# Routed experts of a mixture layer: every gathered block of rows is turned by TensorE instead of every second one by DMA

## The chip, the cores and the metric

The kernel runs on one core of a Trainium2 chip. The metric is the device time of one execution in microseconds (us), lower is better. All times below are of this kernel on that core.

## The reference, cut to what matters

The input is x of 2 x 2048 tokens with 512 features. An attention part comes first (not touched by this change). The feed-forward part is a shared expert plus 16 routed experts, four of them chosen for each token:

```python
g = jnp.einsum('sc,ech->esh', xf, gate_w)      # xf: normalised rows, S=4096, c=512
u = jnp.einsum('sc,ech->esh', xf, up_w)        # 16 experts, h=128
h = jax.nn.silu(g) * u
hw = h * combine.T[:, :, None]                 # zero unless the expert was chosen
routed = jnp.einsum('esh,ehc->sc', hw, down_w)
return (shared_out + routed).reshape(B, T, C)  # added to x
```

## The kernel before

Each of the 4096 tokens goes to 4 experts, which makes 16384 pairs. They are sorted by expert into blocks of 128 rows (P = 128), each block with one expert; with the padding of 16 experts there are at most 143 blocks that can hold a row. The kernel before works through BLOCKS = 144, a multiple of four, so its last block is always padding.

The program has three stretches that matter here. In the first (to about 504 us) there are attention, routing and the shared expert for the first four of eight token blocks. Its last step is `shared_down(FIRST * SH - 1)`. The second is the routed stage, 144 blocks. The third handles the shared expert of the four later token blocks (`gate_up_at`, `down_at`, lines 1015 to 1050) while the routed results y are gathered back by token and added (`combine`).

Values are held as two 16-bit parts, high and low, so a gathered row is 1024 16-bit numbers, and each product takes three matmuls (`PARTS`: high by high, high by low, low by high). The steps of one routed block s are:

- GpSimd gathers 128 rows by token number from DRAM into one of four buffers `xg` (L1832), after copying the token numbers (L1820). The gather waits until the block four before has been turned.
- The block is turned, so that features lie on partitions. Even blocks: eight 128x128 turns on TensorE into a PSUM bank (`turn_rows`, L946), emptied by VectorE into `xgT` (`save_rows`, L1669). Odd blocks: one transposing DMA from `xg` to `xgT_odd`, on SP's queue (`turn_odd`, L576), in order with the y writes (`y_out`, L567).
- TensorE: gate and up, 12 matmuls of 256 columns (`gate_up`, L961), with weights picked by the expert number held in a register.
- ScalarE takes silu of gate (L1269); VectorE multiplies by up (L1683); ScalarE makes the high part (L1273); VectorE the low part (L1686); TensorE turns the two parts (`turn_h`, L972); VectorE empties them (`save_h`, L1675).
- TensorE: down, 3 matmuls of 512 columns (`down`, L980). ScalarE saves y (`save_y`, L1279) into one of two buffers `y_sb`, once the buffer's last write to DRAM is done. SP writes it to `y_dram` (L567).

Order on TensorE: a loop of 34 rounds of four blocks (`four`), with some blocks written out at either end. In a round, for n = 0 to 3 and s = 4i + 1 + n, it does the turns of an even block where n is odd, then gate/up of s + 1, the turns of h of s, and down of s - 1. Each round begins with a load of eight expert numbers into registers (L936). The other engines have loops of four blocks, GpSimd of eight, in matching order.

SP's queue also carries, among the first blocks, the last block of x1 + shared sum to DRAM (`x1s_out(3)`, L484), the DMA transposes of 512 rows of a later token block (`later_turned_in(5)`, L467) and an x1 block in (`next_x1_in(3)`, L480).

Of the kernel before, what the change touches and what calls it, by code (L numbers as in the profile page):

```python
# [27 lines left out]
F16 = mybir.dt.float16  # L28
# [4 lines left out]
P = 128  # L33
# [10 lines left out]
TB = 4  # L44
# [8 lines left out]
BLOCKS = (NP + E * (P - 1)) // P + 1  # L53
# [26 lines left out]
R_EXP, R_BLK, R_TRI = 0, E, E + BLOCKS  # L80
# [3 lines left out]
def constants():  # L84
# [17 lines left out]
    r[:, R_BLK:R_BLK + BLOCKS] = np.arange(BLOCKS)  # L102
# [23 lines left out]
def build(nc, x, ctxT, wk, wqT, wv, wo, biases, bo, cb, routerT, gu_w, dn_w, const, const_r, out):  # L126
    with ExitStack() as ctx:
# [53 lines left out]
        counted = view(o1 + 8 * KB, [BLOCKS])  # L181
# [19 lines left out]
        hot_blk = [view(o2 + 4 * KB + 2 * BLOCKS * TOP_E * i, [TOP_E, BLOCKS], F16) for i in range(3)]  # L201
        hot_blk.append(view(o1 + 8 * KB, [TOP_E, BLOCKS], F16))
# [3 lines left out]
        r_silu, r_h = view(o3 + 8 * KB, [2, H]), view(o3 + 9 * KB, [2, H])  # L206
# [16 lines left out]
        blocks_e = little(BLOCKS + 8, I32)  # L223
# [30 lines left out]
        token_of = little(BLOCKS, I32)  # L254
        pair_row = little(NP // P, F16)
        places16 = little(BLOCKS, F16)
# [90 lines left out]
        s_tx, s_txe = sem("even_rows_turned"), sem("even_rows_turned_saved")  # L347
        s_odd = [sem(f"odd_rows_turned{h}") for h in range(2)]
        s_rg, s_rs, s_rh = sem("routed_gate_up"), sem("routed_silu"), sem("routed_h32")
        s_rhh, s_rhl = sem("routed_h_hi"), sem("routed_h_lo")  # L350
        s_ht, s_hte, s_rd = sem("routed_h_turned"), sem("routed_h_turned_saved"), sem("routed_down")
        s_ye = sem("y_saved")
        s_yw = [sem("y_written0"), sem("y_written1")]
# [22 lines left out]
        def stage_of(n):  # L376

            return n % 2 if n < TB else 2 + n % 2

# [6 lines left out]
        def _(sp):  # L386
# [178 lines left out]
            def y_out(s, j):  # L565
                sp.wait_ge(s_ye, s + 1)
                sp.dma_start(item(y_tiles, s), y_sb[:, j, :]).then_inc(s_yw[j], 16)  # L567


            def turn_odd(h, gathered, used):  # L570

                settled(sp)
                sp.wait_ge(s_xg[2 * h + 1], gathered)
                if used is not None:
                    sp.wait_ge(s_rg, used)
                sp.dma_start_transpose(xgT_odd[:, h, :, :], xg[:, 2 * h + 1, :]).then_inc(s_odd[h], 16)  # L576

            def four_blocks(i):

                loop = not isinstance(i, int)  # L580
                gathered = sp.to_reg(16 * i + 16) if loop else 16 * i + 16
                for h in range(2):
                    used = 4 * i + (2 * h - 2)
                    turn_odd(h, gathered, sp.to_reg(used) if loop else used)
                    for r in (2 * h, 2 * h + 1):
                        y_out(4 * i - 4 + r, r % 2)

            sp.wait_ge(s_shl, FIRST * SH)
            for h in range(2):
                turn_odd(h, 16, None)  # L590

            four_blocks(1)
            x1s_out(FIRST - 1)
            four_blocks(2)
            later_turned_in(FIRST + 1)
            four_blocks(3)
            next_x1_in(FIRST - 1)
            with sp.Fori(4, BLOCKS // 4) as i:
                four_blocks(i)
            for s in range(BLOCKS - 4, BLOCKS):  # L600
                y_out(s, s % 2)
# [4 lines left out]
            for j in range(2):  # L606
                sp.wait_ge(s_yw[j], 16 * BLOCKS // 2)
# [21 lines left out]
        def _(pe):  # L629
# [223 lines left out]
            def tokens(u):  # L853

                for q in range(4):
                    pe.wait_ge(s_hot, 4 * u + q + 1)
                    for i in range(TOP_E):
                        last = mm(bank[6][:, 0:BLOCKS], hot_row[q][:, i, :], hot_blk[q][:, i, :],
                                  start=(u == q == i == 0), stop=(u == SH - 1 and q == 3 and i == TOP_E - 1))
                    last.then_inc(s_hot_used, 1)  # L860
# [64 lines left out]
            shared_down(FIRST * SH - 1)  # L925


            pe.wait_ge(s_sh32, FIRST * SH)
            pe.wait_ge(s_x1s, FIRST * TB)
            pe.wait_ge(s_whi_r, E)  # L930
            pe.wait_ge(s_wlo_r, E)
            pe.wait_ge(s_expert, 1)
# [7 lines left out]
            def turn_rows(u, j, fresh):  # L940

                pe.wait_ge(s_xg[2 * j], 16 * ((u >> 1) + 1))
                if not fresh:
                    pe.wait_ge(s_txe, u - 1)
                for n in range(2 * KC):
                    last = turn(bank16[j][:, n * P:n * P + P], xg[:, 2 * j, n * P:n * P + P], id16)  # L946
                last.then_inc(s_tx, 1)

            def gate_up(s, r, e, fresh):

                j, rows = r % 2, (xgT, xgT_odd)[r % 2]
                if r % 2:
                    pe.wait_ge(s_odd[r // 2], 16 * ((s >> 2) + 1))
                else:
                    pe.wait_ge(s_txe, (s >> 1) + 1)
                if not fresh:
                    pe.wait_ge(s_rh, s - 1)
                n = 0
                for xv, wp in PARTS:
                    for kc in range(KC):  # L960
                        last = mm(bank[2 + j][:, 0:2 * H], rows[:, r // 2, xv * KC + kc, :],  # L961
                                  only((gu_hi_r, gu_lo_r)[wp], e, slice(kc * 2 * H, (kc + 1) * 2 * H)),
                                  start=(n == 0), stop=(n == 3 * KC - 1))
                        n += 1
                last.then_inc(s_rg, 1)

            def turn_h(s, j, fresh):
                pe.wait_ge(s_rhl, s + 1)
                if not fresh:
                    pe.wait_ge(s_hte, s - 1)  # L970
                for v in range(2):
# [3 lines left out]
            def down(s, j, e, fresh):  # L975
                pe.wait_ge(s_hte, s + 1)
                if not fresh:
# [5 lines left out]

            e = experts(0)
            turn_rows(0, 0, True)
            gate_up(0, 0, e[0], True)
            turn_rows(1, 1, True)
            gate_up(1, 1, e[1], True)
            turn_h(0, 0, True)
            def four(i, first):  # L990
                e = experts(4 * i)
                for n in range(4):
                    s = 4 * i + 1 + n
                    if n % 2:
                        turn_rows(2 * i + 2 + n // 2, n // 2, False)
                    gate_up(s + 1, (n + 2) % 4, e[n + 2], False)
                    turn_h(s, (1 + n) % 2, first and n == 0)
                    down(s - 1, n % 2, e[n], first and n < 2)

            four(0, True)  # L1000
            with pe.Fori(1, BLOCKS // 4 - 1) as i:
                four(i, False)
            e = experts(BLOCKS - 4)
            gate_up(BLOCKS - 2, 2, e[2], False)
            turn_h(BLOCKS - 3, 1, False)
# [898 lines left out]
```

## Time and profile before

| what | value |
|---|---|
| median of 3 runs | 1177.35 us (1174.76 to 1182.57) |
| the profiled execution | 1182.4 us, of which the span is 1180.6 us |
| mean granted TensorE clock | 0.945 of full speed |
| TensorE busy | 1049.6 us of the span |
| VectorE busy | 633.7 us |
| ScalarE busy | 385.8 us |
| GpSimd busy | 433.2 us |
| DMA | 227.69 MB, mean 193 GB/s |

The span is counted from the first to the last instruction of the profiled execution; all positions in time below count from its start. PE is TensorE's matmuls, PEld its weight loads (which overlap them), DVE is VectorE, ACT ScalarE, POOL GpSimd, SP the queue that issues most DMAs. A name like L961 is line 961 of the kernel before. The tile names are short: `arena` is all of SBUF that the kernel uses and `bank` any PSUM bank, so the line tells more than the name.

### The profile page before, as it was taken

How to read it: one execution, taken by the hardware profiler on the slowest of the kernel's cores; microseconds unless marked ns; L12 is line 12 of the kernel's file. 1: busy time of each engine (PE TensorE's matmuls, PEld its weight loads, DVE VectorE, ACT ScalarE, POOL GpSimd, SP SyncE). 2: the span in 40 equal slices, each digit the busy share in tenths (PEclk: the TensorE clock that was granted, in tenths of full speed). 3: DMA queues.
4: the chain of work that ended last, by engine and by line, in shares of the span. 5: the costliest groups of instructions: out<-in, count | busy, mean ns of one | idle time of the engine just before them, and what ended most of it. 6: DMA issues, size and time to landing. Idle time of an engine off the chain costs nothing.

```text
span 1180.6 us, 21537 instructions
## 1 busy us (share of the span) xinstructions
PE 1049.6 (89%) x6596; PEld 614.6 (52%) x6597; DVE 633.7 (54%) x1473; ACT 385.8 (33%) x776; POOL 433.2 (37%) x508
## 2 busy tenths in 40 slices
PE   5797979999969688987899999998889789999998
PEld 5494544444424234554666767666666334444443
DVE  5634876655268989832344444444333447565555
ACT  4433423433445343122344444444334011111111
POOL 0303631121225233132344444444431746545440
PEclk8889969999999889988999999999999889999999
DMA  9713754658663324169999999999996966967451
GB/s 358 258 33 104 261 152 137 203 147 248 168 161 108 107 81 134 36 148 243 246 251 255 253 251 255 259 255 235 230 214 180 390 221 166 231 178 212 137 169 42
DMA packets 215318, 227.69 MB, mean 193 GB/s; under 512 B 143682, under 2 KB 152804, under 8 KB 213732
## 3 DMA queue, kind: packets, MB, share of 16 engines
q1 hardware_dynamic: 191716, 149.41, 44.5%
q0 software_dynamic: 23552, 77.61, 23.6%
q8 instruction: 31, 0.51, 0.2%
q14 instruction: 19, 0.16, 0.1%
HBM read 123.93 MB, written 69.49 MB: 164 GB/s over the span
## 4 chain that ended last, share of the span: by engine, by line
PE 65%; DMA 11%; DVE 9%; issue 8%; SPq 4%; ACT 2%; POOL 1%; DVEq 0%; POOLq 0%; ACTq 0%
PE bank L1025 14%; PE bank L961 12%; PE bank L825 10%; PE bank L1037 7%; PE bank L837 6%; PE bank L980 5%; DMA arena<-arena 5%; DMA arena<-xr_dram,arena 3%; PE bank L946 2%; PE bank L713 2%; DVE arena L1647 1%; DMA arena<-in_x 1%; PE bank L635 1%; SPq L467 1%; PE bank L972 1%
## 5 line engine op out<-in xcount | busy, mean ns | idle before, releaser
L961 PE MATMUL bank<-arena 128*128 x1728 | 226.8, 281 | 37.7 <-DMA arena<-arena 20.3
L961 PEld LDWEIGHTS bank<-arena 128*128 128x128 f16 x1728 | 165.4, 99 | 92.1 <-issue 57.4
L825 PE MATMUL bank<-arena 128*128 128x512 f16 x768 | 181.8, 392 | 17.4 <-ACT arena L1213 7.8
L1853 POOL DMA_INDIRECT arena<-y_dram,arena x128 | 131.5, 1027 | 123.7 <-DVE arena L1722 68.8
L1025 PE MATMUL bank<-arena 128*128 128x512 f16 x768 | 174.4, 383 | 2.3 <-issue 1.9
L1832 POOL DMA_INDIRECT arena<-xr_dram,arena x144 | 141.5, 983 | 59.6 <-issue 45.5
L825 PEld LDWEIGHTS bank<-arena 128*128 128x128 f16 x768 | 76.6, 100 | 124.0 <-issue 28.6
L1683 DVE SCALAR_TENSOR_TENSOR arena<-bank,arena 128x128 f32<-128x128 f32 x144 | 42.0, 292 | 179.5 <-ACT arena L1269 134.7
L1025 PEld LDWEIGHTS bank<-arena 128*128 128x128 f16 x768 | 75.5, 98 | 97.8 <-issue 9.0
L980 PE MATMUL bank<-arena 128*128 x432 | 117.9, 382 | 1.7 <-issue 0.8
L1279 ACT ACTIVATE arena<-bank 128x512 f32<-128x512 f32 x144 | 84.8, 589 | 74.8 <-DMA y_dram<-arena 66.7
L1219 ACT ACTIVATE arena<-arena 128x512 f16<-128x512 f32 x64 | 40.4, 631 | 210.2 <-DVE arena L1464 108.4
L1722 DVE SCALAR_TENSOR_TENSOR arena<-arena 128x512 f32<-128x512 f32 x128 | 95.9, 750 | 18.8 <-DMA arena<-y_dram,arena 15.4
L1820 POOL COPY arena<-arena 128x1 int32 (+1 forms) x144 | 27.7, 192 | 204.9 <-DMA arena<-arena 121.5
L1037 PE MATMUL bank<-arena 128*128 128x512 f16 x384 | 90.8, 386 | 9.0 <-issue 9.0
L837 PE MATMUL bank<-arena 128*128 128x512 f16 x384 | 94.7, 400 | 0.0
L1269 ACT ACTIVATE arena<-bank 128x128 f32<-128x128 f32 x144 | 39.8, 277 | 117.6 <-PE bank L961 95.8
L1807 POOL TENSOR_TENSOR arena<-arena 128x1024 f32 x16 | 36.1, 2254 | 102.0 <-ACT arena L1228 91.1
L1686 DVE TENSOR_TENSOR arena<-arena 128x128 f16<-128x128 f32 x144 | 42.3, 293 | 54.3 <-ACT arena L1273 46.7
L1774 POOL TENSOR_TENSOR arena<-arena 128x2048 f16<-128x2048 f32 x7 | 28.5, 4073 | 105.6 <-ACT arena L1168 105.6
L1037 PEld LDWEIGHTS bank<-arena 128*128 128x128 f16 x384 | 38.0, 99 | 55.4 <-issue 12.0
L1730 DVE SCALAR_TENSOR_TENSOR arena<-bank,arena 128x512 f32<-128x512 f32 x32 | 22.1, 691 | 80.3 <-PE bank L1025 57.8
(205 smaller groups left out, 1327.8 us busy)
## 6 DMA issues: line engine op xcount, KB each, us to landing
y_dram<-arena SPq DMA_DIRECT2D x144, 256.0 KB
arena<-in_x SPq DMA_DIRECT2D x8, 1024.0 KB, 14.3
xr_dram<-arena SPq DMA_DIRECT2D x16, 512.0 KB, 3.0
x_dram<-arena SPq DMA_DIRECT2D x8, 1024.0 KB, 4.9
arena<-x_dram SPq DMA_DIRECT2D x8, 1024.0 KB, 6.0
arena<-in_gu_w SPq DMA_DIRECT2D x16, 512.0 KB, 3.4
out<-arena SPq DMA_DIRECT2D x32, 256.0 KB
arena<-in_gu_w POOLq DMA_DIRECT2D x8, 512.0 KB, 3.9
```

Source lines behind the costliest of these rows:

```text
L825: last = mm(bank[half][:, :], (gu_hi_s, gu_lo_s)[wp][:, c, at:at + H], xt[:, xv * KC + kc, :], start=(n == 0), stop=(n == 3 * KC - 1))
L837: last = mm(bank[2 + t][:, :], s_hb[:, g % 2, hv, t * P:t * P + P], (dn_hi_s, dn_lo_s)[wp][:, c, :], start=(c == 0 and n == 0), stop=(c == ...
L961: last = mm(bank[2 + j][:, 0:2 * H], rows[:, r // 2, xv * KC + kc, :], only((gu_hi_r, gu_lo_r)[wp], e, slice(kc * 2 * H, (kc + 1) * 2 * H) ...
L980: last = mm(bank[6 + j][:, :], r_hT[:, j, hv, :], only((dn_hi_r, dn_lo_r)[wp], e), start=(n == 0), stop=(n == 2))
L1025: last = mm(bank[GATE_UP[n % 2][g]][:, :], (gu_hi_s, gu_lo_s)[wp][:, c, at:at + H], xt[:, xv * KC + kc, :], start=(m == 0), stop=(m == 3 * ...
L1037: last = mm(bank[2 + t][:, :], s_hb[:, n % 2, hv, t * P:t * P + P], (dn_hi_s, dn_lo_s)[wp][:, c, :], start=(c == 0 and m == 0), stop=(c == ...
L1279: A(y_sb[:, j, :], bank[6 + j][:, :], ACT.Copy, scale=1.0 / WS).then_inc(s_ye, 1)
L1683: V.scalar_tensor_tensor(r_h[:, j, :], bank[2 + j][:, H:2 * H], 1.0 / WS, r_silu[:, j, :], ALU.mult, ALU.mult).then_inc(s_rh, 1)
L1686: V.tensor_tensor(r_hb[:, j, 1, :], r_h[:, j, :], r_hb[:, j, 0, :], ALU.subtract).then_inc(s_rhl, 1)
L1722: V.scalar_tensor_tensor(acc, ybuf[n % RING][:, e, :], w, acc, ALU.mult, ALU.add).then_inc(s_cmb, 1)
L1832: pool.indirect_dma_start(out=xg[:, r % 4, :], out_offset=None, in_=xr_dram[:, :], in_offset=bass.IndirectOffsetOnAxis(ap=token_now[:, r:r ...
L1853: pool.indirect_dma_start(out=ybuf[n % RING][:, e, :], out_offset=None, in_=y_dram[:, :], in_offset=bass.IndirectOffsetOnAxis(ap=row_of[:, ...
```

## The change

- Every gathered block is turned by TensorE, and VectorE empties each. The DMA transposes of the routed stage, `xgT_odd` and their semaphores go.
- On TensorE the turns of block s + 2 come ahead of gate/up of s + 1, the turns of h of s, and down of s - 1. The turns of blocks 0 and 1 come ahead of the last shared down projection. The first gate/up groups wait for the first quarters of the shared sum rather than for all.
- TensorE's routed stage has no loop; it is written out block by block, and loads the expert numbers every eighth block.
- y has four buffers instead of two. Two of them lie where the shared expert's silu is kept, so ScalarE waits for their last writes ahead of the last stage.
- 143 blocks instead of 144; tables of block numbers keep an even number of columns.
- The loops of ScalarE, VectorE, GpSimd and SP have eight blocks a round.

```diff
-BLOCKS = (NP + E * (P - 1)) // P + 1
+BLOCKS = (NP + E * (P - 1)) // P
+COLUMNS = BLOCKS + BLOCKS % 2
+UNROLLED = 8
+LOOPED = BLOCKS // UNROLLED - 1
...
-        xgT_odd = view(o1, [2, 2 * KC, P], F16)
-        y_sb = view(o3 + 4 * KB, [2, D])
+        y_sb = [view(v, [D]) for v in (o1, o3 + 4 * KB, o3 + 6 * KB, o1 + 2 * KB)]
...
-                sp.dma_start_transpose(xgT_odd[:, h, :, :], xg[:, 2 * h + 1, :]).then_inc(s_odd[h], 16)
...
+            for s in range(UNROLLED):
+                y_out(s, s % 4)
+                if s == 3:
+                    x1s_out(FIRST - 1)
+                    later_turned_in(FIRST + 1)
+                if s == 7:
+                    next_x1_in(FIRST - 1)
+            with sp.Fori(1, LOOPED + 1) as i:
+                for n in range(UNROLLED):
+                    y_out(UNROLLED * i + n, n % 4)
...
+            def turn_rows(s):
+
+                pe.wait_ge(s_xg[s % 4], 16 * (s // 4 + 1))
+                if s >= 2:
+                    pe.wait_ge(s_txe, s - 1)
+                for n in range(2 * KC):
+                    last = turn(bank16[s % 2][:, n * P:n * P + P], xg[:, s % 4, n * P:n * P + P], id16)
                 last.then_inc(s_tx, 1)
...
-            e = experts(0)
-            turn_rows(0, 0, True)
-            gate_up(0, 0, e[0], True)
...
-            four(0, True)
-            with pe.Fori(1, BLOCKS // 4 - 1) as i:
-                four(i, False)
...
+            turn_rows(0)
+            pe.wait_ge(s_sh32, FIRST * SH)
+            turn_rows(1)
+            shared_down(FIRST * SH - 1)
+            pe.wait_ge(s_expert, 1)
+            of = {s: e for s, e in enumerate(experts(0))}
+            gate_up(0, of[0])
+            for s in range(BLOCKS + 1):
+                if s + 2 < BLOCKS:
+                    turn_rows(s + 2)
+                if s + 1 < BLOCKS:
+                    gate_up(s + 1, of[s + 1])
+                if s % 8 == 5 and s + 3 < BLOCKS:
+                    of.update(enumerate(experts(s + 3), s + 3))
+                if s < BLOCKS:
+                    turn_h(s)
+                if s:
+                    down(s - 1, of[s - 1])
...
-            def gather(s, r, fresh, last):
-
-                if not fresh:
-                    if r % 2:
-                        pool.wait_ge(s_odd[r % 4 // 2], 16 * (s >> 2))
-                    else:
-                        pool.wait_ge(s_tx, (s - 2) >> 1)
+            def gather(s, r):
+
+                if not isinstance(s, int) or s >= 4:
+                    pool.wait_ge(s_tx, s - 3)
```

## Rows read from the trace of the kernel before

**Rows 1.** Stretches: us, busy us (instructions) by engine, granted clock, DMA share, GB/s
```profile
504.40:580.00 75.60, 56.95 (x443) 41.66 (x444) 24.91 (x75) 21.64 (x60) 24.64 (x43) 0.86 0.87 207
580.00:800.00 220.00, 206.95 (x1796) 151.42 (x1794) 93.48 (x300) 94.83 (x257) 100.62 (x173) 1.00 0.97 255
800.00:908.70 108.70, 94.79 (x792) 68.51 (x791) 41.14 (x133) 42.52 (x115) 38.31 (x64) 0.97 0.89 221
908.70:1180.60 271.90, 255.39 (x1152) 113.30 (x1150) 147.77 (x208) 39.70 (x65) 131.47 (x128) 0.97 0.65 192
```

**Rows 2.** Chain that ended last, 703 to 716 us: start us, us, what
```profile
703.09 0.45 PE bank L946 x8
703.54 1.31 PE bank L961 x12
704.85 0.11 PE bank L972 x2
704.96 0.65 PE bank L980 x3
705.61 0.51 issue
706.12 1.59 PE bank L961 x12
...
715.56 0.75 issue
```

**Rows 3.** Line 936, the register loads: duration ns min/median/max, first and last start
```profile
L936 PEldq TENSOR_LOAD <-arena x37: 587/712/1406, 507.0 to 900.7; - x37
```

**Rows 4.** Waits of TensorE, 504 to 909 us: us in total, times, longest
```profile
PE bank L961 <- DMA arena<-arena: 20.3, 8, 5.0
...
PE bank L961 <- DVE arena L1683: 3.7, 7, 0.8
PE bank L946 <- issue: 3.5, 1, 3.5
PE bank L961 <- DVE arena L1669: 1.9, 2, 1.0
PE bank L972 <- DVE arena L1686: 1.8, 4, 0.7
```

**Rows 5.** Order of time on TensorE, one group behind a DMA wait
```profile
569.67 2.74 PE L961 MATMUL bank<-arena 128*128 x12 [4.30 <-DMA arena<-arena]
```

**Rows 6.** DMA queues, 580 to 800 us: packets, MB, share of 16 engines
```profile
q1 hardware_dynamic: 57703, 33.68, 58.2%
q0 software_dynamic: 6829, 22.35, 38.7%
```

**Rows 7.** Chain that ended last, two gathers from issue to landing
```profile
528.52 9.52 DMA arena<-xr_dram,arena
...
683.17 4.33 DMA arena<-xr_dram,arena
```

**Rows 8.** Groups by line, 504 to 909 us: busy, mean ns, idle before and its releasers
```profile
L1279 ACT ACTIVATE arena<-bank 128x512 f32<-128x512 f32 x143 | 84.2, 589 | 72.6 <-DMA y_dram<-arena 64.5 <-PE bank L980 4.0 <-remote 2.0
L1669 DVE COPY arena<-bank 128x1024 f16<-128x1024 f16 x72 | 49.1, 683 | 8.7 <-PE bank L946 6.8 <-PE bank L961 1.6 <-issue 0.2
...
L1686 DVE TENSOR_TENSOR arena<-arena 128x128 f16<-128x128 f32 x144 | 42.3, 293 | 54.3 <-ACT arena L1273 46.7 <-issue 7.5
L1683 DVE SCALAR_TENSOR_TENSOR arena<-bank,arena 128x128 f32<-128x128 f32 x144 | 42.0, 292 | 179.5 <-ACT arena L1269 134.7 <-issue 44.7
L1675 DVE COPY arena<-bank 128x256 f16<-128x256 f16 x144 | 40.8, 284 | 1.0 <-PE bank L972 1.0
```

**Rows 9.** Page, parts 1 and 3: busy us and instructions; instruction queue, packets, MB, share
```profile
PE 1049.6 (89%) x6596; PEld 614.6 (52%) x6597; DVE 633.7 (54%) x1473; ACT 385.8 (33%) x776; POOL 433.2 (37%) x508
...
q8 instruction: 31, 0.51, 0.2%
```

**Rows 10.** Chain that ended last, first gate/up of the last stage
```profile
908.69 10.36 PE bank L1025 x48
```

More of the change, by code:

```diff
@@ L78 @@
 C_END = C_T + NA * P
[L80 removed]
+R_EXP, R_BLK, R_TRI = 0, E, E + COLUMNS
 R_END = R_TRI + P
@@ L378, in stage_of, with written @@
             return n % 2 if n < TB else 2 + n % 2
+        def written(r):
+            return 16 * len(range(r, BLOCKS, 4))
         def settled(engine):
@@ L562, in _, with y_out @@
             later_turned_in(FIRST)
-            def y_out(s, j):
+            def y_out(s, r):
                 sp.wait_ge(s_ye, s + 1)
[L567 to L575, printed above, removed]
-                sp.dma_start_transpose(xgT_odd[:, h, :, :], xg[:, 2 * h + 1, :]).then_inc(s_odd[h], 16)
[L578 to L601, printed above, removed]
+                sp.dma_start(item(y_tiles, s), y_sb[r]).then_inc(s_yw[r], 16)
+            for s in range(UNROLLED):
[8 more added lines that the diff above has]
+                    y_out(UNROLLED * i + n, n % 4)
+            for s in range(UNROLLED * (LOOPED + 1), BLOCKS):
+                y_out(s, s % 4)
             sp.wait_ge(s_rd, BLOCKS)
             sp.wait_ge(s_x1sw, 16 * FIRST)
-            for j in range(2):
-                sp.wait_ge(s_yw[j], 16 * BLOCKS // 2)
+            for r in range(4):
+                sp.wait_ge(s_yw[r], written(r))
             for k in range(FIRST):
@@ L947, in turn_rows, with gate_up @@
                 last.then_inc(s_tx, 1)
-            def gate_up(s, r, e, fresh):
-                j, rows = r % 2, (xgT, xgT_odd)[r % 2]
-                if r % 2:
-                    pe.wait_ge(s_odd[r // 2], 16 * ((s >> 2) + 1))
-                else:
[L955 to L964, printed above, removed]
+            def gate_up(s, e):
+                j = s % 2
+                pe.wait_ge(s_txe, s + 1)
+                if s >= 2:
+                    pe.wait_ge(s_rh, s - 1)
+                else:
+                    pe.wait_ge(s_x1s, (FIRST - 1) * TB + j + 1)
+                for n, (xv, wp, kc) in enumerate((xv, wp, kc) for xv, wp in PARTS for kc in range(KC)):
+                    last = mm(bank[2 + j][:, 0:2 * H], xgT[:, j, xv * KC + kc, :],
+                              only((gu_hi_r, gu_lo_r)[wp], e, slice(kc * 2 * H, (kc + 1) * 2 * H)),
+                              start=(n == 0), stop=(n == 3 * KC - 1))
@@ L1281, in _ @@
-            silu_hi(0, 0, True)
-            silu_hi(1, 1, True)
-            with act.Fori(0, BLOCKS // 4 - 1) as i:
-                for n in range(4):
-                    silu_hi(4 * i + 2 + n, n % 2, False)
-                    save_y(4 * i + n, n % 2, 2 * i + n // 2)
-            for n in range(2):
-                silu_hi(BLOCKS - 2 + n, n, False)
-                save_y(BLOCKS - 4 + n, n, BLOCKS // 2 - 2)
-            for n in range(2):
-                save_y(BLOCKS - 2 + n, n, BLOCKS // 2 - 1)
+                if not isinstance(before, int) or before:
+                    act.wait_ge(s_yw[n % 4], 16 * before)
@@ new lines, in save_y @@
+                A(y_sb[n % 4], bank[6 + n % 2][:, :], ACT.Copy, scale=1.0 / WS).then_inc(s_ye, 1)
+            silu_hi(0, 0)
+            for s in range(UNROLLED):
+                silu_hi(s + 1, s + 1)
+                if s:
+                    save_y(s - 1, s - 1, (s - 1) // 4)
+            with act.Fori(1, LOOPED + 1) as i:
+                for n in range(UNROLLED):
+                    silu_hi(UNROLLED * i + n + 1, n + 1)
+                    save_y(UNROLLED * i + n - 1, n + 7, UNROLLED // 4 * i + (n - 1) // 4)
@@ L1294, in _ @@
+            for s in range(UNROLLED * (LOOPED + 1), BLOCKS + 1):
+                if s + 1 < BLOCKS:
+                    silu_hi(s + 1, s + 1)
+                save_y(s - 1, s - 1, (s - 1) // 4)
+            for r in (0, 3):
+                act.wait_ge(s_yw[r], written(r))
             for n in LAST:
@@ L1836, in _ @@
             copy_tokens(0, 0)
[L1837 to L1846 removed]
+            for s in range(UNROLLED):
+                gather(s, s)
+            with pool.Fori(1, LOOPED + 1) as i:
+                for r in range(UNROLLED):
+                    gather(UNROLLED * i + r, r)
+            for s in range(UNROLLED * (LOOPED + 1), BLOCKS):
+                gather(s, s % 8)
+            for r in range(4):
+                pool.wait_ge(s_yw[r], written(r))
             pool.wait_ge(s_rd, BLOCKS)
```

176 lines of the change are left out of this document (71 added, 105 removed).

## The prediction

> **What bounds the kernel now.** Read the stretches first: what each engine did in the routed stage, from the end of the last shared down projection (504.4 us) to the start of the last gate/up work (908.7 us), and before and behind it. TensorE is busy most of the time in all of it and DMA is almost full in the middle: from 580 to 800 us PE has 206.95 of 220 us, DMA a share of 0.97 at 255 GB/s and the granted clock is 1.00 [rows 1]. So two resources run near their limit together, and a change that moves work from one to the other can lose as well as gain. The question is what one block costs TensorE when nothing holds it up.
>
> That stands in the chain of work, where each piece counts from the end of the piece before: 0.45 us for the eight turns of a gathered block, 1.31 for the twelve gate/up matmuls, 0.11 for the two turns of h, 0.65 for the three down matmuls [rows 2]. A block without turns is 2.07 us, one with turns 2.52. (The durations of the grouped rows, 273 to 383 ns a matmul, overlap each other and can't be summed.) Then look at the seam: at every fourth block there are 0.51 or 0.75 us of "issue", and the gate/up work behind it takes 1.59 instead of 1.31 us [rows 2]. That is 0.8 to 1.05 us per round, the branch together with the load of eight expert numbers into registers; the load alone is 0.71 us, 37 times [rows 3].
>
> Then the waits of TensorE: 20.3 us for the DMA transposes in 8 pieces, up to 5.0 us each; 3.5 us once ahead of the first turn; 3.7 + 1.9 + 1.8 = 7.4 us for VectorE [rows 4]. A stall costs more than itself: behind one of 4.3 us the twelve gate/up matmuls took 2.74 us, twice 1.31 with the pipeline's end, so the clock had fallen to its lower level, 1.2 GHz [rows 5]. The clock was 0.86 from 504.4 to 580 us and 0.97 from 800 us on [rows 1]: (1 - 0.86) x 75.6 + 0.03 x 108.7 = 13.9 us of work at the upper level. Part of that fell on idle time; I take 10.
>
> The stage of before adds up: 144 x 2.07 = 298.1; 72 x 0.45 = 32.4; 36 seams at 0.9 = 32.4; DMA waits 20.3; VectorE 7.4; start 3.5; clock 10. Sum 404.1, measured 908.7 - 504.4 = 404.3. The accounting may be off inside its soft terms (seam and clock), but nothing large is missing. **TensorE's stream sets the stage, and DMA adds stalls to it.**
>
> **The change, part by part.**
>
> *Turns.* The 72 DMA transposes go, TensorE turns all 143 blocks: 143 x 0.45 = 64.4 us, +32.0. None of it is hidden, since TensorE is the bound. The first two are done ahead of the last shared down projection, which only moves them. This is the known cost of the change.
>
> *One block fewer.* The last block is all padding: -2.07 us (its turn is counted above).
>
> *Seams.* 36 seams, 32.4 us, go with the loop. What stays are 17 register loads inside the stage (at s = 5, 13, ..., 133), set between a gate/up group and the turns of h. How much of a load is exposed is not shown alone. Lower bound: a load takes 0.71 us [rows 3] and TensorE had 0.11 + 0.65 us of queued work in front of the seam [rows 2], so nearly 0; I set 0.2. Upper bound: a whole seam, 0.9. I take 0.5 (in a seam, 0.51 us of idle are left with a branch in it), 8.5 us, with 3.4 and 15.3 as ends. Gain 23.9.
>
> *DMA.* Per block there remain one gather and one y write, 256 KB each. In the full stretch the hardware queue (y writes and transposes, 33.68 MB) had a share of 58.2% and the software queue (gathers, 22.35 MB) 38.7% [rows 6]: 1.73% a MB in both. So a transposed MB costs DMA what another costs, and what is removed is worth its bytes. Two blocks have five transfers of 256 KB (two gathers, two writes, one transpose), of which four stay: 0.97 x 4/5 = 0.78 at the same pace of blocks. So DMA stops being full, and its queues get short.
> What is late next is the gather. Ring of four rows: gather s + 4 is released by the end of turn s and must be there for turn s + 4, that is 4 x 2.52 - 0.45 = 9.6 us, less about 0.7 until its issue. From issue to landing it took 4.3 us in the full stretch and 9.5 in the crowded start [rows 7]. The first fits twice over; the second just misses. The crowd at the start stays (x1s out, the transpose of 512 rows of a later token block, x1 in, 1 MB each), and is now put into the first 8 blocks, on SP's queue between y writes; a y write behind them waits, and four y buffers give it 10 us. I leave 5 us of DMA stall (0 to 20.3) and 4 us of clock (0 to 10).
>
> *Four y buffers.* ScalarE waited for the y writes 64.5 us in all [rows 8], in front of the next silu, since its queue is in order. Of that TensorE saw only its waits for VectorE, which stands behind silu: part of 7.4 us. I leave 2 (0 to 7.4), the end of the pipeline being in it.
>
> *VectorE.* It now empties a turned block in every block: 0.683 + 0.292 + 0.293 + 0.284 = 1.55 us, and about 0.32 us in which it waits for ScalarE between two of them (46.7 us / 144) [rows 8]. 1.9 us in a period of 2.52. The emptied rows are wanted a block later, so this stays hidden; had VectorE needed over 2.5 us, it would be the new bound. Its loop, ScalarE's and GpSimd's go from four (or eight) blocks a round to eight; 0.6 us of slack a block takes a seam of theirs.
>
> *Start.* The 3.5 us of idle ahead of the first turn [rows 4] were a wait for all of the shared sum, with the first register load behind it, at 507.0 us [rows 3]. Now the turns don't wait for it, and the first gate/up waits only for its first quarter: 1 us stays (0 to 3.5).
>
> *Behind the stage* y gathers wait for the last y write, as before. One wait is added: two of the y buffers lie where the last stage keeps its silu, so ScalarE waits for the last writes from them ahead of its first silu there, and VectorE and the first down group wait behind it. That group comes only after 48 gate/up matmuls, 10.36 us [rows 10], while a y write takes a few; I cost it at nothing, and without that cover at the few. I take the 271.9 us behind 908.7 [rows 1] as they are.
>
> *Sum:* 296.0 + 64.4 + 8.5 + 5 + 4 + 2 + 1 = 380.9 against 404.3: -23.4 us. The profiled execution took 1182.4 us (span 1180.6), which becomes 1159.0. The median of the runs is 1177.35, 5 us less than the profiled one, and I forecast 1177.35 - 23.4 = **1154 us**. With the good ends together (3.4, 0, 0, 0, 0) the stage is 364 us and the time 1137; with loads at 15.3, 10 of stall, 8 of clock, 5 and 2 it is 401 and the time 1174. Not all ends meet: 1143 to 1170 for this case.
>
> **The rivals.**
>
> *The stalls stay.* If the DMA waits come from gathers and writes in bursts rather than from the transposes, 20.3 + 10 + 7.4 stay, and the stage is 296.0 + 64.4 + 8.5 + 1 + 37.7 = 407.6: 1181 us, no difference one can tell. For it: the 9.5 us gather, and the clock of 0.86 at the start, where the extra 3 MB are. Against: every DMA wait of TensorE ended with a transpose, none with a gather [rows 4], and a transpose had to wait for its gather first, two trips in a row within one ring of four. Chance 0.14.
>
> *Slower: TensorE's instructions don't come fast enough.* Written out, the stage has 143 x 50 = 7150 matmuls and weight loads, where before the loop was fetched once. Before: 13193 executed less 33 repeats of 168 is 7650 in the program, and one instruction queue moved 0.51 MB in 31 packets [rows 9]; if that is TensorE's, it is 67 bytes for one of these, and 14300 of them give 58 packets, 27 more. At the new pace (50 in 2.52 us, 20 a us) a packet is used up in 12 us, on DMA engines 78% full. Were each 2 us late, that is +54 us: 1208 us. It decides from 23.4 / 27 = 0.87 us a packet. Against: the stretch from 908.7 us on is written out too and has 2302 of these in 271.9 us with PE 94% busy [rows 1], but at 8.5 a us, not 20. Chance 0.10. The Trainium skill speaks against this rival (Runtime: NRT & Kernel Launch, Instruction fetch mechanics): fetch is sequential and ahead of use, and a taken branch is what breaks it; by it the case has no cost. No row here shows a dense written-out stretch of this length.
>
> *Slower: the clock.* Turns would be 0.56 of 2.52 us (22%) instead of 13%. If they did not hold the clock up, all of it would run at the lower level, where gate/up took 2.74 [rows 5]: 2.52 becomes 5.04 us, +360 us, 1514. Against: the clock stayed 1.00 for 220 us with turns in the mix and 13 us of idle [rows 1]. Chance 0.03. The Trainium skill has the rule (TensorE: Matmul & The Clock Gate, Part 4: PE-mode transpose): transposes don't count as busy in the same way; by the trace they are at least diluted enough now.
>
> **How the numbers follow.** Forecast 0.73 (1154, 1143 to 1170), stalls stay 0.14 (1181), fetch 0.10 (1208), clock 0.03 (1514). To leave no more than 2 in 10 out, the range goes from 1143 up to the case in which the stalls stay, 1181: 0.13 lies above it by the slow rivals, and some 0.05 below or between. About 1%, 11.8 us, is what a measurement of this kernel can tell. Faster by more than that: 0.73 less its weak end 0.05, 0.68. Within: 0.05 + 0.14 = 0.19. Slower: 0.13.
>
> **What the profile of after would show.** Starts of gate/up groups 2.52 us apart between 580 and 800 us, DMA share near 0.78, clock 1.00; 18 register loads, with a gap of 0.2 to 0.9 us each; ScalarE's wait for y writes near 0; the stage near 381 us. If gate/up waits for the emptied rows on VectorE, that step is wrong; if turns wait for gathers by more than some 5 us, the ring step is; idle "issue" every 12 us is the fetch rival; a clock below 0.95 in the middle is the clock rival. A tail other than 272 us would be an effect I have not costed.

## Result: faster by 2.9%, more than forecast

The changed kernel took 1140.78 us (median of 4 runs, 1138.82 to 1146.03), the kernel before 1176.05 us beside it (4 runs). The ratio is 0.9713, with a 95% interval of 0.9639 to 0.9786. That is 34 us less, against 23.4 forecast. It lies 2 us below the stated range of 1143 to 1181. Some executions run in a slower state; the ratios leave them out, the medians don't.

The profile after, first by stretches (us, busy us and instructions of PE, PEld, DVE, ACT, POOL, granted clock, DMA share, GB/s):

```profile
480.00:501.90 21.90, 21.89 (x125) 10.79 (x123) 16.70 (x46) 2.45 (x4) 7.97 (x13) 1.00 0.21 59
501.90:580.00 78.10, 72.64 (x706) 57.82 (x707) 41.28 (x115) 29.13 (x82) 31.83 (x56) 0.98 0.72 220
580.00:800.00 220.00, 219.59 (x2180) 176.18 (x2178) 121.31 (x348) 93.69 (x262) 101.45 (x175) 1.00 0.64 209
800.00:870.30 70.30, 69.68 (x679) 55.08 (x677) 38.00 (x111) 30.41 (x85) 25.61 (x44) 1.00 0.58 195
870.30:1139.20 268.90, 254.33 (x1153) 113.33 (x1150) 147.62 (x208) 39.62 (x66) 130.91 (x128) 0.98 0.66 194
```

Against [rows 1]: the routed stage is 368.4 us (501.9 to 870.3) instead of 404.3, the last stage 268.9 instead of 271.9, and the last shared down projection ends at 501.9 instead of 504.4 us although two blocks' turns now stand in front of it. The spans differ by 41.4 us, of which the stage is 35.9. The profiled run of before was one of its slower ones, so the medians differ by less.

TensorE is busy for 219.59 of 220 us. The chain of work that ended last, in the middle (start us, us, what), is one unbroken row of pieces, and so it goes on for 220 us:

```profile
701.58 0.45 PE bank L922 x8
702.03 1.31 PE bank L934 x12
703.34 0.11 PE bank L948 x2
703.45 0.65 PE bank L958 x3
704.10 0.45 PE bank L922 x8
```

The period is 2.52 us (the gate/up groups start at 702.03 and 704.55), the sum of [rows 2] to the hundredth. There is no gap where a register load stands. One was issued at 704.1, within these lines. All loads of the run (duration ns min/median/max, first and last start):

```profile
L912 PEldq TENSOR_LOAD <-arena x18: 587/592/779, 498.8 to 845.8; - x18
```

TensorE's waits from 501 to 871 us answer to [rows 4] (us in total, times, longest):

```profile
PE bank L948 <- DVE arena L1659: 3.1, 2, 2.5
PE bank L922 <- DMA arena<-xr_dram,arena: 2.0, 1, 2.0
PE bank L934 <- DVE arena L1451: 1.0, 1, 1.0
PE bank L948 <- issue: 0.4, 1, 0.4
```

So the 31 us of waits in [rows 4] became 6.5, and 4.5 of those are two waits near 530 and 538 us, where the three large transfers are. The DMA queues of 580 to 800 us (packets, MB, share), against [rows 6], and TensorE's likely instruction queue of the whole run against [rows 9]:

```profile
q0 software_dynamic: 6962, 22.81, 36.2%
q1 hardware_dynamic: 12563, 22.88, 27.2%
```

```profile
q8 instruction: 64, 1.05, 0.4%
```

The written-out stream doubled the instructions fetched (31 packets to 64, against 27 more forecast), without a gap.

### The profile page after: what moved, and what is told of

The parts are those of the page before. It is cut to its first block, busy times and chain, and to the rows that moved or that the text cites. A ratio compares the mean times of both kernels' runs of the same rounds, so it can differ in the third digit from the quotient of the medians.

```text
span 1139.2 us, 22052 instructions
## 1 busy us (share of the span) xinstructions
PE 1049.0 (92%) x7147; PEld 642.1 (56%) x7147; DVE 675.5 (59%) x1541; ACT 379.9 (33%) x773; POOL 429.4 (38%) x506
## 4 chain that ended last, share of the span: by engine, by line
PE 78%; DVE 10%; issue 4%; DMA 3%; ACT 2%; SPq 2%; DVEq 0%; ACTq 0%
PE bank L934 16%; PE bank L995 15%; PE bank L809 11%; PE bank L958 8%; PE bank L1007 7%; PE bank L821 6%; PE bank L922 5%; PE bank L697 2%; DVE arena L1625 2%; PE bank L948 1%; PE bank L619 1%; SPq L472 1%; PE bank L643 1%; PE bank L633 1%; DVE arena L1403 1%
## 5 line engine op out<-in xcount | busy, mean ns | idle before, releaser
L934 PE MATMUL bank<-arena 128*128 x1716 | 211.2, 273 | 1.0 <-DVE arena L1451 1.0
L934 PEld LDWEIGHTS bank<-arena 128*128 128x128 f16 x1716 | 161.8, 98 | 18.5 <-issue 1.6
L809 PEld LDWEIGHTS bank<-arena 128*128 128x128 f16 x768 | 76.8, 101 | 123.0 <-issue 29.3
L995 PEld LDWEIGHTS bank<-arena 128*128 128x128 f16 x768 | 75.1, 98 | 97.0 <-issue 7.3
L958 PE MATMUL bank<-arena 128*128 x429 | 116.1, 379 | 0.0
L1647 DVE COPY arena<-bank 128x1024 f16<-128x1024 f16 x143 | 97.5, 682 | 4.5 <-PE bank L922 3.6
L922 PEld LDWEIGHTS bank<-arena 128*128 128x128 f16 x1144 | 76.0, 97 | 35.7 <-DMA arena<-xr_dram,arena 2.4
L922 PE MATMUL bank<-arena 128*128 128x128 f16 x1144 | 87.6, 219 | 2.0 <-DMA arena<-xr_dram,arena 2.0
```

Source lines behind the costliest of these rows:

```text
L809: last = mm(bank[half][:, :], (gu_hi_s, gu_lo_s)[wp][:, c, at:at + H], xt[:, xv * KC + kc, :], start=(n == 0), stop=(n == 3 * KC - 1))
L922: last = turn(bank16[s % 2][:, n * P:n * P + P], xg[:, s % 4, n * P:n * P + P], id16)
L934: last = mm(bank[2 + j][:, 0:2 * H], xgT[:, j, xv * KC + kc, :], only((gu_hi_r, gu_lo_r)[wp], e, slice(kc * 2 * H, (kc + 1) * 2 * H)), sta ...
L958: last = mm(bank[6 + j][:, :], r_hT[:, j, hv, :], only((dn_hi_r, dn_lo_r)[wp], e), start=(n == 0), stop=(n == 2))
L995: last = mm(bank[GATE_UP[n % 2][g]][:, :], (gu_hi_s, gu_lo_s)[wp][:, c, at:at + H], xt[:, xv * KC + kc, :], start=(m == 0), stop=(m == 3 * ...
L1647: V.tensor_copy(xgT[:, j, :, :], bank16[j].rearrange("p (n q) -> p n q", n=2 * KC)).then_inc(s_txe, 1)
```

## Experiments

Each ran beside the kernel before on the same chip; ratios are to that. "The changed kernel" is 0.9713 in these terms, or 1140.8 us. It was not run again beside the experiments, and the medians of the kernel before in the four sets lie between 1169 and 1181 us, so a difference to the changed kernel is good to some 10 us. Finer is the length of the routed stage in each run's profile, from the end of the last shared down projection to the first gate/up of the last stage, though each is one execution (us):

| kernel | routed stage | last stage |
|---|---|---|
| before | 404 | 272 |
| changed | 368 | 269 |
| odd blocks by DMA | 409 | 262 |
| every fourth by DMA | 398 | 268 |
| loop of eight, load one value off | 418 | 266 |
| load in each block | 524 | 262 |
| load in each block, aligned | 367 | 268 |
| loads one block earlier | 377 | 262 |
| loop of eight, aligned | 381 | 270 |
| loop of four | 376 | 270 |
| two y buffers | 373 | 263 |
| before with four y buffers | 393 | 261 |
| transfers spread | 361 | 261 |
| and late sum | 361 | 256 |

### Undoing the turns: odd blocks by DMA again

```diff
+            # SP, ahead of the y write of block s - 5, for odd s; buffers where the shared expert's h was
+                sp.wait_ge(s_xg[r % 4], gathered)
+                sp.wait_ge(s_rg, used)
+                sp.dma_start_transpose(xgT_dma[:, h, :, :], xg[:, r % 4, :]).then_inc(s_dt[h], 16)
...
+                if s % 8 in DMA_TURNED:       # (1, 3, 5, 7); TensorE's turn_rows and VectorE's save_rows
+                    return
```

> The changed kernel, but the 71 odd blocks are turned by DMA as before; the written-out stream, four y buffers and 143 blocks stay. Theory A (TensorE's stream sets the pace, a transposed MB costs DMA what another does, so DMA has room at 0.8): TensorE needs 2.295 us a block, 32 us faster than the changed kernel, if few stalls come back. Theory C (a DMA transpose takes 1.8 us of all 16 DMA engines against 0.9 for a gather and 0.7 for a y write, so DMA is full at 2.5 us a block): DMA share 0.97 or more, TensorE waits for transposes, and the time is between 5 us faster and 15 us slower than the changed kernel.

Measured: 1178.46 us, ratio 1.0081 (1.0044 to 1.0118). This is the whole gain given back and slightly more, though the written-out stream, the four buffers and the 143 blocks are all there and TensorE has 32 us less work than in the changed kernel. Its waits (500 to 900 us) and the stretch from 580 to 800 us:

```profile
PE bank L992 <- DMA arena<-arena: 49.4, 26, 15.7
```

```profile
580.00:800.00 220.00, 202.85 (x1724) 149.71 (x1723) 90.20 (x288) 89.23 (x246) 95.42 (x164) 0.98 0.98 245
```

TensorE waits for transposes, and around 700 us the chain is made of DMA trips. 23.0 of the 49.4 us lie ahead of 580 us, 15.7 in one wait at 543 us, beside the large transfers; from 580 to 800 us its 1724 matmuls, at 21 a block, are 82 blocks, 2.68 us each. Theory A fell. What TensorE saves by handing turns over, the transposes take back, at least in this order of SP's queue: the edit issues them elsewhere than the kernel before did, and what that costs by itself was not tested (the run with four buffers in the kernel before, below, bears on it).

### Every fourth block by DMA

The same edit with the residues (3, 7).

> The changed kernel, but every fourth block (residues 3 and 7 of eight) is turned by DMA, the other three by TensorE. From the traces a gather is 0.91 us of all 16 DMA engines, a y write 0.68, a transpose 1.8: 2.05 us a block, and TensorE needs 2.07 + 0.75 x 0.45 = 2.41 us. Theory C (DMA's own time decides): TensorE stays the bound, 35 x 0.45 = 16 us faster than the changed kernel, 10 to 16 with a few stalls. Theory I (the trip of gather and transpose in a row, 4 + 6.5 us within a ring of four, decides even when DMA has room): TensorE waits for transposes, and no gain or a loss of up to 20 us.

Measured: 1185.46 us, ratio 1.0034 (0.9971 to 1.0097). Half as many transposes, and still all of the gain is gone. DMA is not full here: its share is 0.88 from 580 to 800 us. TensorE waits 25.0 us for transposes, in 16 pieces, and once 9.3 us for a gather at the start. The chain from 718 to 741 us shows what holds:

```profile
718.50 5.54 DMA arena<-arena
...
724.95 3.79 DMA arena<-xr_dram,arena
...
728.79 7.67 DMA arena<-arena
...
737.38 4.00 DMA arena<-xr_dram,arena
```

A buffer of the ring is gathered into (3.8 us), transposed out of (5.5 to 7.7 us), and only then free for the next gather; with 0.9 us to release it and issue, 724.95 to 737.38 is one round, 12.4 us. The ring has four buffers, each used once in four blocks, which TensorE would do in 4 x 2.41 = 9.6 us. Theory I holds: **the two trips in a row within the ring set the pace, with DMA at 0.88**. In the run before this, a round was 700.63 to 712.20, 11.6 us. GpSimd waits 68.4 us of 220 for the release by a transpose here and 66.2 in the kernel before; that alone proves nothing, since in the changed kernel, which is not held by its ring, it waits 72.2 us for TensorE's turns. Why a transpose takes 5.5 to 8.5 us from issue to landing I did not take apart.

### Undoing the written-out stream

First, a loop of eight blocks a round with a load of ten values at the top:

```diff
+            with pe.Fori(1, LOOPED + 1) as i:
+                e = experts(UNROLLED * i - 1)          # ten values
+                for n in range(UNROLLED):
+                    s = UNROLLED * i + n
+                    turn_rows(s + 2, n + 2, 2 * i + (n + 2) // 4 + 1)
+                    gate_up(s + 1, n + 1, e[n + 2])
+                    turn_h(s, n)
+                    down(s - 1, n + 1, e[n])
```

> The changed kernel, but TensorE's routed stage is a loop of eight blocks a round (16 rounds) with one register load at the top of each. Theory A (the seam of 0.8 to 1.05 us is the taken branch with a load behind it, and nothing is queued ahead across it): 16 seams, 13 to 17 us slower than the changed kernel. Theory B (a seam costs what a load costs, so with loads hidden it is hidden too): no change. If the DMA relief alone had made the gain, also no change.

Measured: 1190.66 us, ratio 1.0178 (1.011 to 1.0246), 50 us slower than the changed kernel, some three times what theory A gave. The seam (start us, us, what) and the loads:

```profile
717.09 2.06 issue
719.15 0.98 PE bank L922 x8
720.13 2.56 PE bank L934 x12
```

```profile
L912 PEldq TENSOR_LOAD <-arena x19: 1277/2673/2745, 501.7 to 902.7; - x19
```

The 16 seams have 31.2 us of idle, up to 2.1 each, and behind this one the turns and gate/up take 0.98 + 2.56 instead of 0.45 + 1.31 us, at the lower clock: 3.8 us in all. The load of ten values takes 2.7 us, where that of eight took 0.59 in the changed kernel. To see why, I compared with a run that loads in each block:

```diff
-                if s % 8 == 5 and s + 3 < BLOCKS:
+                if s >= 5 and s + 3 < BLOCKS:
                     of.update(enumerate(experts(s + 3), s + 3))
```

> The changed kernel, but TensorE loads the expert numbers in every block from the fifth on: 134 more register loads, 0.59 us each. Theory A (in a written-out stream a load is hidden: the sequencer needs less than the array's 2.52 us a block): no change, within 3 us of the changed kernel. Theory B (my forecast's 0.5 us a load, wherever it stands; bounds 0.2 and 0.9): 27 to 120 us slower than the changed kernel, 67 at 0.5.

Measured: 1296.23 us, ratio 1.108 (1.1005 to 1.1155), 155 us slower, outside both theories (the stage is 155 us longer too). Taken one by one, these loads take 0.59, 2.2, 2.2, 2.2 us and again 0.59: in order of blocks, the short ones are those that begin at value 8, 12, 16, 20. Two in a row, each from the view of one line in a window of 3 or 4 us, and the gap behind the slow one:

```profile
L912 PEldq TENSOR_LOAD <-arena x1: 2184/2184/2184, 702.5 to 702.5; - x1
...
L912 PEldq TENSOR_LOAD <-arena x1: 593/593/593, 706.6 to 706.6; - x1
```

```profile
703.64 1.17 issue
```

That gave the rule to test: a load of 4-byte values that begins at a multiple of four values takes 0.59 us for eight, any other 0.27 us a value. The changed kernel's loads begin at multiples of eight. Two runs put it to the test, one with as many loads as before in good places, one with as few as in the changed kernel in bad ones:

```diff
+                    at = (s + 3) // 8 * 8            # a load in each block, all at a multiple of eight
+                    of.update(enumerate(experts(at), at))
```

> The changed kernel with a load of eight values in every block from the fifth on, as in the first run, but always at a multiple of eight values. Theory A with the address rule (a load at a multiple of four takes 0.59 us and TensorE's queue covers it): at most 5 us slower than the changed kernel. Theory B (the count of loads matters, whatever the address): over 27 us slower.

```diff
-                if s % 8 == 5 and s + 3 < BLOCKS:
+                if s % 8 == 4 and s + 3 < BLOCKS:    # begins at 7, 15, 23, ...
```

> The changed kernel with as many loads as it has (17 in the stage, one in eight blocks), each one block earlier and so one value below a multiple of eight. Theory A with the address rule (such a load takes 2.2 us instead of 0.59, and TensorE's queue covers 1 to 1.3 us of it, as in the run with a load in each block): 17 gaps of 0.9 to 1.3 us, 15 to 22 us slower than the changed kernel. Theory J (one slow load in eight blocks is covered, only many in a row are not): within 4 us of the changed kernel.

The first: 1138.74 us, ratio 0.966 (0.9593 to 0.9726), so 119 loads cost nothing. The second: 1147.73 us, ratio 0.984 (0.9743 to 0.9937), 7 us slower than the changed kernel by the medians and 9 in the stage; its interval reaches that kernel's, but its trace shows the cause:

```profile
L912 PEldq TENSOR_LOAD <-arena x18: 783/1983/2319, 502.0 to 854.6; - x18
```

```profile
PE bank L948 <- issue: 6.9, 16, 0.6
```

16 gaps of 0.4 us, and 0.3 us of slower start behind each (0.27 + 0.82 instead of 0.11 + 0.65 us). That is less than expected, since more of a load is covered: the load at 708.3 us starts 1.8 us before TensorE's queued work ends (710.10), where with a load in each block that at 702.5 starts 1.1 us before (703.64). My reading is that the queue fills up within eight blocks and does not within one. So the address rule stands, and the rival J is half right.

With the load in its place, the loop again, of eight and of four blocks:

```diff
+            with pe.Fori(1, 33 + 1) as i:
+                e = experts(4 * i)                   # loop of eight: 8 * i, ten values
+                for n in range(1, 4 + 1):
+                    s = 4 * i + n
```

> The loop of eight again, but its one load (ten values) starts at a multiple of four values, where the loads of the run before it that took 0.59 us started, not one value off, where they took 2.2 to 2.7 us. Theory F (what made the loop of eight 50 us slower was mostly the misplaced load, 2.7 us against 0.6, and the clock that fell behind each 2.1 us gap): gaps under 1 us, no fall of the clock, 16 seams of 0.5 to 1.05 us, 8 to 17 us slower than the changed kernel. Theory G (a round of eight blocks, some 400 matmuls and weight loads, is too long for TensorE's instruction memory, so that each branch back waits for a fetch): still gaps of 2 us and 35 to 50 us slower.

> The changed kernel, but TensorE's routed stage is a loop of four blocks a round as in the kernel before (33 rounds), with one load of eight values at a multiple of four at the top of each; all blocks are turned by TensorE. Theory A (seam 0.8 to 1.05 us, as in the kernel before): 26 to 35 us slower than the changed kernel, so about the time of the kernel before, and the written-out stream would be worth all of the gain. Theory H (the kernel before was held by DMA at 2.5 us a block and its seams were partly hidden behind that; a seam is the branch alone and the load is overlapped): 10 to 25 us slower.

Measured: the loop of eight 1159.25 us, ratio 0.9868 (0.9781 to 0.9954), 18 us slower than the changed kernel; the loop of four 1154.43 us, ratio 0.9828 (0.9741 to 0.9914), 14 us slower. In the stage it is 13 and 8 us. Theory F holds in the first: 31 of the 50 us were the misplaced load and the clock. Its 16 seams are 1.0 us each, though (0.67 us of idle and 0.34 of slower start); its loads of ten values take 1.36 us (median), and I can't tell that from the length of the round. In the loop of four a seam is this (start us, us, what):

```profile
708.95 0.65 PE bank L958 x3
709.59 0.20 issue
709.80 0.62 PE bank L922 x8
710.41 1.34 PE bank L934 x12
```

0.20 + 0.17 + 0.03 = 0.4 us, 33 times 13.2: by its number theory H, and less than half of the seam of [rows 2]. In this loop the turns stand behind the load, though; in the kernel before it is the gate/up work, which needs the loaded numbers. What that order is worth was not run by itself.

### The y buffers, in both kernels

```diff
-        y_sb = [view(v, [D]) for v in (o1, o3 + 4 * KB, o3 + 6 * KB, o1 + 2 * KB)]
+        y_sb = [view(v, [D]) for v in (o3 + 4 * KB, o3 + 6 * KB) * 2]
-                    act.wait_ge(s_yw[n % 4], 16 * before)
+                    act.wait_ge(s_yw[(n + 2) % 4], 16 * before)    # the write two blocks before
```

> The changed kernel, but with two y buffers. Theory A (ScalarE's 64.5 us of waits for y writes came from full DMA queues, and were hidden but for the start): up to 6 us slower, all of it in the first 15 blocks where the transpose of a later token block holds SP's queue for 8 us. Theory D (the second pair of buffers made a large part of the gain): 10 us slower or more, spread over the stage.

Measured: 1141.63 us, ratio 0.978 (0.9715 to 0.9845). The median is the changed kernel's, the stage 4 us longer: theory A. ScalarE waits 12.3 us for y writes instead of none, 10.9 of them in one wait behind the large transfers. And the other way round, four buffers in the kernel before:

```diff
-        y_sb = view(o3 + 4 * KB, [2, D])
+        y_sb = [view(v, [D]) for v in (o3 + 4 * KB, o3 + 6 * KB, o1 + 4 * KB, o1 + 6 * KB)]
```

> The kernel before with four y buffers and nothing else changed. Theory C (the ring of gather and DMA transpose holds it, the waits for y writes are beside the path): within 8 us of the kernel before. Theory D (ScalarE's 64 us of waits held up silu and with it TensorE): 10 to 25 us faster, and much of the change's gain would be its buffers.

Measured: 1158.12 us, ratio 0.9865 (0.9793 to 0.9938), 16 us faster. Theory C fell here, and D has the number. So the waits of ScalarE that I took to be beside the path were partly on it. TensorE's waits, 500 to 910 us:

```profile
PE bank L961 <- issue: 18.6, 28, 1.3
PE bank L961 <- DMA arena<-arena: 17.0, 7, 5.1
```

Of the waits of [rows 4] those for the hidden values (3.7 + 1.8) all but went; gate/up no longer stands behind a silu that is late. What is left is the seam. From 640 to 760 us the chain is TensorE's alone, and at every fourth block it has this (start us, us, what):

```profile
690.57 0.53 issue
691.11 1.62 PE bank L961 x12
...
700.58 0.57 issue
701.15 1.60 PE bank L961 x12
```

The seven seams from 690.57 to 751.49 are 10.15 us apart in the mean, 0.97 more than 4 x 2.07 + 2 x 0.45. So the seam of [rows 2] is TensorE's own in this order of work, and no wait for silu or a transpose.

Against the run with odd blocks by DMA, this one has the same four buffers and as many transposes a block, and its stage is 16 us shorter (393 and 409) although it has the seams and that one has none. So turning by DMA can go at 2.53 us a block (1829 matmuls from 580 to 800 us); the 2.68 there belongs in part to that edit's order of transfers.

The two edits don't add up: the buffers alone give 16 us, and with two buffers the rest of the change gives 26 by the ratio beside its own kernel before, or all 34 by the medians.

### A better version

```diff
-            for s in range(UNROLLED):
+            for s in range(3 * UNROLLED):
                 y_out(s, s % 4)
                 if s == 3:
                     x1s_out(FIRST - 1)
-                    later_turned_in(FIRST + 1)
-                if s == 7:
+                if s == 11:
+                    later_turned_in(FIRST + 1)
+                if s == 19:
                     next_x1_in(FIRST - 1)
```

> The changed kernel with the three large transfers at the start of the routed stage taken apart on SP's queue: x1 + shared sum out behind the y write of block 3 as before, the transpose of a later token block behind that of block 11 instead of 3, and x1 in behind that of block 19 instead of 7. Theory K (the stalls of TensorE near 530 to 540 us, 2.0 + 2.5 us and a lower clock for some us, come from their meeting): no such stalls, 4 to 7 us faster than the changed kernel. Theory L (the transpose alone does it, as it holds SP's queue for 8 us): the stall moves and the time stays.

```diff
-                for p in range(c * len(mine) // SH, (c + 1) * len(mine) // SH):
+                late = k == FIRST
+                for p in range(max(c - late, 0) * len(mine) // (SH - late), (c + 1 - late) * len(mine) // (SH - late)):
                     combine(mine[p])
```

> As the run before it, and in the last stage VectorE adds the first gathered y one step later, so that the second hidden step of the shared expert doesn't stand behind the wait for the first y gathers. Theory K with it: the 4.3 us wait of TensorE at the start of the last stage goes too, 8 to 11 us faster than the changed kernel. Rival: the sum that is put off is missing at the end of that token block and the wait comes back there; then as the run before it.

Measured: 1133.59 us, ratio 0.9687 (0.9612 to 0.9761), and 1126.89 us, ratio 0.9627 (0.9551 to 0.9703). The second is 14 us below the changed kernel by the medians, 10 by the ratios. In its trace TensorE's waits in the routed stage are down to two (500 to 872 us), and 580 to 800 us is full:

```profile
PE bank L935 <- DVE arena L1452: 1.0, 1, 1.0
PE bank L949 <- DVE arena L1660: 0.6, 1, 0.6
```

```profile
580.00:800.00 220.00, 220.00 (x2190) 176.80 (x2188) 121.58 (x350) 94.36 (x264) 101.92 (x175) 1.00 0.65 210
```

The wait of 4.5 us at the start of the last stage, which the run without the late sum still has, is gone. Theory K holds for both. The last stage is 5.5 us shorter with the second edit (256 us against 261), 7 by the medians: the wait, and the clock, which in the first 60 us of that stage is granted at 0.94 without the late sum and at 1.00 with it.

## Why the prediction was too small

**What was right.** The direction, and the period: 2.07 + 0.45 = 2.52 us a block, read from [rows 2], is what was measured. TensorE's own work, 359.5 us without the two turns that lie ahead of 501.9, is 98% of the stage of 368.4. The price of a seam, 0.9 us, is near what the kernel before with four y buffers shows (0.97). VectorE hid the emptying of every block. The gathers and their ring gave one wait of 2.0 us. The start and the ends cost what was left for them (1 + 2). The fetch rival and the clock rival did not come: 33 more packets without a gap, and a clock of 1.00 with turns at 22% of the time. On the clock the rule of the Trainium skill would have had turns fail to hold it up (TensorE: Matmul & The Clock Gate, Part 4: PE-mode transpose); in this mix the trace shows no such effect.

**The step that failed** is the price of the register loads that stay, in *Seams*: 0.5 us each, 8.5 in all, with a lower end of 0.2. Measured: 0, in the changed kernel and again with 119 loads. It is 8.5 of the 12.5 us by which the stage was shorter than forecast (368.4 against 380.9); the stalls, ends and clock, for which I left 12, came to 8.9 and 0.9 of the turns was counted twice (it lies ahead of 501.9). The rows had said it: 0.76 us of queued work in front of a load of 0.71. I took the idle time of a seam, where a branch stands in front of the load and work that needs it behind, as a measure of a load inside a stream. That the loads stood at good addresses was luck that I hadn't seen: one block off, each showed 0.4 us of gap and 0.3 of slower start.

**A term that was too small for the kernel before** is the y buffers. I charged ScalarE's 64.5 us of waits with at most 7.4 on TensorE. Four buffers in the kernel before gave 16 us by the medians and 11 in the stage of the profiles; in the changed kernel the second pair is worth 4 us in the stage. So for this change the sum is not far off, but "part of 7.4 us" is wrong as a price of those waits.

**How far "TensorE's stream sets the stage, and DMA adds stalls to it" holds.** For the kernel before it holds: its blocks from 580 to 800 us are 2.57 us each (1796 matmuls), TensorE with its seams takes 2.54 (10.15 us for four). It does not hold for the next step. With the seams taken out TensorE would want 2.3 us a block with half of the turns at DMA and 2.41 with a fourth, and neither run was faster: the round trip of gather and transpose through the ring of four took 11.6 and 12.4 us in the pieces looked at. DMA, at 0.97 to 0.99 of its time, had next to no room below TensorE's 2.54 us, and in these runs the seams could be cashed in only together with the transposes. I had written that a transpose waits for its gather, two trips in a row, but used it only against a rival. Whether some other order of the transposes, without seams, would beat the changed kernel stays open.

**DMA.** I expected a share of 0.78 and it is 0.64. From 27.2% for 22.88 MB a y write is 0.69 us of all 16 engines; in before 85 y writes at that price leave 70 us of the hardware queue's 128 for 43 transposes: 1.6 us each, 2.3 times a y write of the same size, where I had set them equal. This takes the y writes of before to cost what they cost after. The equality of the two queues in [rows 6] was a mean of cheap writes and dear transposes. The packets point the same way: [rows 6] has 57703 for the hardware queue where the changed kernel has 12563, nearly all of y writes, so a transpose is some 1050 packets and a y write of the same size 144.

**The remainder**, 3.0 us in the last stage and 2.5 ahead of the routed one, is within what these stretches do by themselves. In the kernels that leave the work of the last stage alone it takes 261 to 272 us (the table), with or without a second group of gaps of TensorE 31 to 44 us into it; and what is ahead of the routed stage, the same in the changed kernel and in all its variants, ends anywhere from 502 to 510 us. So a part of the 2 us by which the range was missed can be that.

## What to carry to other kernels

Price an instruction where it will stand: a register load behind a branch was part of a 0.9 us seam, the same load inside a full stream cost nothing. A sum of parts that closes does not say what one edit will give: where two resources run at nearly the same pace, taking work from one alone gave nothing here. Two DMA trips in a row through a ring cost their latency, and not only their bytes, so compare the round trip with the ring's period before reading the DMA share. When loop variables pick table entries by register, align the load, and put it inside the stream, away from the branch.

## What the runs showed of the hardware

- A load of eight 4-byte values from SBUF into TensorE's registers took 0.59 us inside a written-out stream where it began at a multiple of four values, and mostly 1.9 to 2.3 us elsewhere (ten values in a loop: 1.36 and 2.7 us). Behind the branch of a loop the aligned load of eight took 0.59 to 1.7 us, with medians of 0.71 to 0.87.
- The Trainium skill has about 200 ns a register even for bulk, for `TENSOR_LOAD`s that the runtime puts in (Runtime: NRT & Kernel Launch, Instruction fetch mechanics). The misplaced loads, 0.27 us a value, are near that, the aligned ones at 0.074 are not.
- TensorE's queue hid 0.59 us in each of 119 blocks, but for 0.7 us in all; of loads of 2.0 us (median), eight blocks apart, it left 0.4 us of gap, and of loads of 2.2 us in each block 1.2 (where looked at).
- Behind gaps of 2.06 us, on a stream otherwise full, gate/up took 2.56 instead of 1.31 us, the lower level of the clock (mean 0.94 from 580 to 800 us); behind the gaps of the aligned loop of eight, 0.65 to 0.70 us, it stayed at 1.00.
- A DMA transpose of 128x1024 16-bit values within SBUF took 4.3 to 8.4 us from issue to landing in the pieces looked at of the two runs that turn by DMA without a loop (DMA share 0.88 and 0.98), and 4.6 and 4.9 us in the kernel before near 680 us.
